# Self-attention: the value product of the first half of the keys in three split terms, and the value bias added where attended values leave PSUM

## The reference, cut to what matters

```
q = (h @ wq + bq), k = (h @ wk + bk), v = (h @ wv + bv)      # 16 heads of 128
q = q * cos + _rotate_half(q) * sin                          # k alike
scores = jnp.einsum('bhqd,bhkd->bhqk', q, k) / math.sqrt(HD)
scores = jnp.where(causal[None, None], scores, jnp.finfo(jnp.float32).min)
probs = jax.nn.softmax(scores.astype(jnp.float32), axis=-1).astype(q.dtype)
out = jnp.einsum('bhqk,bhkd->bhqd', probs, v)
return out.transpose(0, 2, 1, 3).reshape(b, s, H * HD) @ wo + bo
```

## Time and profile before

| | us |
|---|---|
| median of three runs | 1918.01 |
| profiled execution | 1916.59 |
| span of its trace | 1914.5 |
| mean granted TensorE clock | 0.962 of full |
| busy: TensorE / ScalarE / VectorE / GpSimd | 1746.0 / 1314.5 / 1090.2 / 1069.3 |
| the self-attention stage, about | 418 to 1012 |

### The profile page before, as it was taken

One profiled execution on the slowest core, in us unless ns is written; L12 is line 12 of the kernel. 1 busy time (PEld: TensorE's weight loads), 2 busy tenths in 40 slices (PEclk: granted clock), 3 DMA queues, 4 the chain that ended last, 5 costly groups with the idle time before them and its releaser, 6 DMA issues.

```text
span 1914.5 us, 36598 instructions
## 1 busy us (share of the span) xinstructions
PE 1746.0 (91%) x11648; PEld 1571.9 (82%) x11648; DVE 1090.2 (57%) x3109; ACT 1314.5 (69%) x4238; POOL 1069.3 (56%) x1187
## 2 busy tenths in 40 slices
PE   4499999449999999999998997999999999999798
PEld 1388888338999999999987885888888888888797
DVE  1477777556666666566775555455555555565222
ACT  1277778248888888888884443788888888888221
POOL 1433334379988889889962113444544544554364
PEclk9699999759999999999998998999999999999899
DMA  3000001110000000000002000000000000000000
GB/s 113 23 17 18 15 21 34 53 33 12 18 23 12 18 23 12 18 18 12 18 7 77 19 28 7 8 12 11 8 12 8 11 12 11 20 14 14 4 23 23
DMA packets 28384, 40.23 MB, mean 21 GB/s; under 512 B 4770, under 2 KB 18338, under 8 KB 27940
## 3 DMA queue, kind: packets, MB, share of 16 engines
q1 hardware_dynamic: 28196, 37.90, 6.6%
HBM read 33.69 MB, written 4.19 MB: 20 GB/s over the span
## 4 chain that ended last, share of the span: by engine, by line
PE 68%; ACT 13%; issue 5%; POOL 4%; DVE 4%; DMA 1%; POOLq 0%; SPq 0%; ACTq 0%; DVEq 0%
PE pS L947 4%; PE pF L508 4%; PE pF L510 4%; PE pF L509 4%; ACT pA L1562 4%; PE pA L510 3%; PE pA L509 3%; PE pA L508 3%; PE pA L939 3%; PE pA L938 3%; PE pA L940 3%; PE pO L966 3%; PE pF L679 3%; PE pS L658 3%; ACT x_P L1588 2%
## 5 line engine op out<-in xcount | busy, mean ns | idle before, releaser
L508 PE MATMUL pA<-Wh,XTh 128*128 128x512 f32 (+1 forms) x512 | 221.5, 433 | 5.6 <-DVEq L117 2.9
L1310 POOL TENSOR_TENSOR f_sw<-f_sw,f_sin 128x512 f32<-128x512 f32 x128 | 179.9, 1406 | 40.6 <-ACT f_sw L1059 40.6
L510 PE MATMUL pA<-Wh,XTl 128*128 128x512 f32 (+1 forms) x512 | 188.7, 369 | 0.0
L509 PE MATMUL pA<-Wl,XTh 128*128 128x512 f32 (+1 forms) x512 | 188.6, 368 | 0.0
L1059 ACT ACTIVATE f_sw<-pA 64x512 f32<-64x512 f32 x256 | 152.0, 594 | 37.3 <-PE pA L940 33.5
L938 PE MATMUL pA<-XTh,Wh 128*128 128x256 f32 x512 | 163.1, 319 | 10.9 <-DMA wg<-in_w_gate 10.3
L1313 POOL TENSOR_TENSOR f_sw<-f_sw,f_RB 128x512 f32<-128x512 f32 x128 | 166.9, 1304 | 10.0
L1588 ACT ACTIVATE x_P<-x_P,x_nm 128x192 f32<-128x192 f32 (+1 forms) x256 | 128.8, 512 | 35.8 <-DVE x_nm L1704 35.8
L503 POOL TENSOR_TENSOR Wl<-RAW,Wh 128x256 fp32r<-128x256 f32 (+3 forms) x64 | 61.0, 952 | 159.9 <-ACT Wh L496 159.9
L939 PE MATMUL pA<-XTl,Wh 128*128 128x256 f32 x512 | 145.4, 284 | 0.0
L940 PE MATMUL pA<-XTh,Wl 128*128 128x256 f32 x512 | 145.3, 284 | 0.0
(11 more groups left out here) (275 smaller groups left out, 6093.7 us busy)
## 6 DMA issues: line engine op xcount, KB each, us to landing
RAW<-in_w_f SPq DMA_DIRECT2D x32, 256.0 KB, 2.7
RAW<-in_w_x SPq DMA_DIRECT2D x32, 160.0 KB, 2.2
RAW<-in_w_x SPq DMA_DIRECT2D x32, 128.0 KB, 2.0
RAW<-in_w_ff SPq DMA_DIRECT2D x8, 288.0 KB, 2.8
R<-in_x SPq DMA_DIRECT2D x4, 512.0 KB, 5.9
x_spill<-R SPq DMA_DIRECT2D x1, 2048.0 KB, 7.5
RAW<-in_w_moe SPq DMA_DIRECT2D x8, 256.0 KB, 2.6
moe_xs<-x_spill SPq DMA_DIRECT2D x8, 256.0 KB, 3.1
```

The costliest lines, as they stand in the source:

```text
L508: e.matmul(o, ah, bh, start=first, stop=False)
L509: e.matmul(o, ah, bl, start=False, stop=False)
L510: return e.matmul(o, al, bh, start=False, stop=last)
L1310: e.tensor_tensor(y, y, bc(sind[:, :], 1, 2), ALU.mult).then_inc(q["swm"], 1)
```

## The change

The value product over the first 128 keys is done as three split products, in place of one float32 product; the one over the last 128 keys stays as it is. For that the probabilities of those keys (PTh, PTl) and V of the first 128 positions (Vh, Vl) are kept as high and low parts. ScalarE's `p_ev` becomes two copies (PTh with 256 columns, PT1 with 128). VectorE gets a new step `p_low` for each head, which makes PTl from pT and PTh; `take(i,4)` becomes a copy to Vh and a subtraction to Vl, `take(i,5)` a plain copy. `attend` now waits for pl, raised by `p_low`, and no longer for te. The bias of V is added in `o_ev` and `o_low`, from a table bv of one column for each head that is loaded once ahead of the stage instead of four broadcast loads.

```diff
@@ attend (TensorE)
-                    e.wait_ge(q["te"], at_p(i, h) + 1)
+                    e.wait_ge(q["pl"], HG * i + h + 1)
...
-                    e.matmul(pO[:, 0:S], V[:, i % 2, 0, v], PT[:, h % 2, 0:S], start=True, stop=False)
-                    e.matmul(pO[:, P:S], V[:, i % 2, 1, v], PT[:, h % 2, S:S + P], start=False, stop=True
+                    three(e, pO[:, 0:S], Vh[:, i % 2, v], Vl[:, i % 2, v], PTh[:, h % 2, :], PTl[:, :], True, False)
+                    e.matmul(pO[:, P:S], V1[:, i % 2, v], PT1[:, h % 2, :], start=False, stop=True
                              ).then_inc(q["pv"], 1)
@@ p_tr (TensorE); norm_tr and logits get the same wait
                     e.wait_ge(q["te"], pos(c - 1))
+                    if c >= 2:
+                        e.wait_ge(q["pl"], lows(c))
@@ p_ev and o_ev (ScalarE)
-                    e.activation(PT[:, h % 2, :], pT[:, c % 2, 0:SW], ACT.Copy).then_inc(q["te"], 1)
+                    e.activation(PTh[:, h % 2, :], pT[:, c % 2, 0:S], ACT.Copy)
+                    e.activation(PT1[:, h % 2, :], pT[:, c % 2, S:SW], ACT.Copy).then_inc(q["te"], 1)
...
-                    e.activation(OTh[:, i % 2, h, :], pO[:, 0:S], ACT.Copy).then_inc(q["oth"], 1)
+                    x = (i // 8) * HG + h
+                    e.activation(OTh[:, i % 2, h, :], pO[:, 0:S], ACT.Identity, bias=bv[:, x:x + 1]
+                                 ).then_inc(q["oth"], 1)
@@ take, n = 4 and 5 (VectorE)
-                        e.tensor_tensor(V[:, i % 2, n - 4, :], pA[:, n % 2, :], bv[:, g % 2, :], ALU.add
+                        if n == 5:
+                            e.tensor_copy(V1[:, i % 2, :], pA[:, n % 2, :]).then_inc(q["taken"], 1)
+                            return
+                        e.tensor_copy(Vh[:, i % 2, :], pA[:, n % 2, :]).then_inc(q["vh"], 1)
+                        e.wait_ge(q["vh"], i + 1)
+                        e.tensor_tensor(Vl[:, i % 2, :], pA[:, n % 2, :], Vh[:, i % 2, :].bitcast(F32), ALU.subtract
                                         ).then_inc(q["taken"], 1)
@@ o_low and p_low (VectorE)
-                    e.tensor_tensor(OTl[:, i % 2, h, :], pO[:, 0:S], OTh[:, i % 2, h, :].bitcast(F32),
-                                    ALU.subtract).then_inc(q["ot"], 1)
+                    x = (i // 8) * HG + h
+                    e.scalar_tensor_tensor(OTl[:, i % 2, h, :], pO[:, 0:S], bv[:, x:x + 1],
+                                           OTh[:, i % 2, h, :].bitcast(F32), ALU.add, ALU.subtract
+                                           ).then_inc(q["ot"], 1)
+
+                def p_low(i, h):
+                    c = at_p(i, h)
+                    e.wait_ge(q["te"], c + 1)
+                    e.wait_ge(q["pv"], HG * i + h)
+                    e.tensor_tensor(PTl[:, :], pT[:, c % 2, 0:S], PTh[:, h % 2, :].bitcast(F32), ALU.subtract
+                                    ).then_inc(q["pl"], 1)
@@ VectorE's list of an iteration
                     soft(i, 2)
+                    p_low(i, 0)
                     w_high(i)
...
                         take(j, 3)
                         take(j, 4)
+                    p_low(i, 1)
                     w_low(i)
...
                         soft(j, 0)
+                    p_low(i, 2)
...
                         recip(j, 1)
+                    p_low(i, 3)
```

More of the change, by code:

```diff
@@ L859, in self_attention @@
             bqk = sb(name + "_bqk", [P, 4, NH], F32, scope)
-            bv = sb(name + "_bv", [P, 2, GW], F32, scope)
+            bv = sb(name + "_bv", [P, NH], F32, scope)
             RB = sb(name + "_RB", [P, 2, 2 * NT, S], F32, scope)
@@ L864, in self_attention @@
             kT = sb(name + "_kT", [P, 2, HG, S], F32, scope)
-            V = sb(name + "_V", [P, 2, T, GW], F32, scope)
+            Vh = sb(name + "_Vh", [P, 2, GW], F32R, scope)
+            Vl = sb(name + "_Vl", [P, 2, GW], F32R, scope)
+            V1 = sb(name + "_V1", [P, 2, GW], F32, scope)
             PB = sb(name + "_P", [P, HG, SW], F32, scope)
@@ L869, in self_attention @@
             rs = sb(name + "_rs", [P, HG, T], F32, scope)
-            PT = sb(name + "_PT", [P, 2, SW], F32, scope)
+            PTh = sb(name + "_PTh", [P, 2, S], F32R, scope)
+            PTl = sb(name + "_PTl", [P, S], F32R, scope)
+            PT1 = sb(name + "_PT1", [P, 2, P], F32, scope)
             OTh = sb(name + "_OTh", [P, 2, HG, S], F32R, scope)
@@ L876, in self_attention @@
             names = ("nhi", "nlo", "raw0", "raw1", "hi", "split", "proj", "taken", "sw", "swm", "swb", "rb", "rope", "tr", "te", "sc", "sct",
-                     "ex", "rs", "pn", "pv", "oth", "ot", "f", "acc", "const", "bias0", "bias1")
+                     "ex", "rs", "pn", "pv", "oth", "ot", "f", "acc", "const", "pl", "vh")
             q = {x: sem(f"{name}_{x}") for x in names}
             raw_in = [q["raw0"], q["raw1"]]
-            bias_in = [q["bias0"], q["bias1"]]
             turns = []
@@ L892, in at_p, with lows @@
                 return place["p", i, h]
+            def lows(c):
+                return sum(x[0] == "p" for x in turns[:c - 1])
             def sp(e):
@@ L897, in sp @@
                 e.dma_start(mask[:, :], d["mask_f0"]).then_inc(q["const"], 16)
+                e.dma_start(bv[:, :], d["f0_bv"]).then_inc(q["const"], 16)
                 e.dma_start(bqk[:, :, :].rearrange("p a n -> p (a n)"), d["f0_bqk"]).then_inc(q["const"], 16)
                 e.dma_start(wg[:, :, :].rearrange("p k e -> p (k e)"), d["w_gate"]).then_inc(q["const"], 16)
[L901 to L905, removed]
                 for i in range(NI):
                     g = i // 8
-                    if i % 8 == 1 and g < G - 1:
-                        e.wait_ge(q["taken"], NQ * 8 * g)
-                        biases(g + 1)
                     if g == G - 1:
@@ L995, in logits @@
                     ins.then_inc(q["tr"], 1)
-                e.wait_ge(q["const"], 80)
+                e.wait_ge(q["const"], 96)
                 for n in range(NQ):
@@ L2519, in layout @@
                                        rows(a[f0 + "wo"][g * GW:(g + 1) * GW])], 1) for g in range(G)])
-    o["f0_bv"] = a[f0 + "bv"]
+    o["f0_bv"] = col(a[f0 + "bv"])
     bqk = np.concatenate([col(a[f0 + "bq"]), col(a[f0 + "bk"])], 1)
```

2 lines of the change are left out of this document (removed).

## The result

| | before | after |
|---|---|---|
| median of the runs, us | 1918.39 (1918.01 to 1922.36, 4 runs) | 2078.82 (2077.20 to 2081.00, 4 runs) |
| profiled execution, us | 1916.6 | 2078.91 |
| its span, us | 1914.5 | 2077.1 |
| mean granted TensorE clock | 0.962 | 0.942 |

The change makes the kernel slower: ratio 1.0832 (95% interval 1.0813 to 1.0851). Forecast: 2066, range 2013 to 2096.

A forecast was written before the change was run, and what follows sets the result against it. The self-attention stage was taken to run at TensorE's own pace (busy 182.00 of 182.00 us). 1916.6 - 9.7 + 81.5 + 36.6 + 4 + 0.5 = 2029.5, with 1.4 to the median 2031, plus 35 for the clock 2066; range 2013 to 2096.

The forecast's parts named there:

- Head 1: Value product waits for p_low behind take(j,3), take(j,4); T is its transposes' start; stall 2.63 us, 81.5 over 31 iterations.
- Head 3: Value product waits for p_low behind recip(j,1), which waits for ScalarE's exp; stall 1.18 us, 36.6 over 31 iterations.
- Heads 0 and 2, reserve 0.15, no stall: p_low right behind a softmax pass ends at T + 2.16 to 2.21, product due at T + 2.4.
- TensorE's saving, 9.7 us: Three split products of 0.118 us replace a 0.43 step: 0.076 us a head, 9.7 over 128 heads.
- The clock, 21 x 1.7 = 35 us: TensorE's clock falls behind head 1's gap in two of three iterations, 1.7 us each; bounds 0 and 53.
- Rival B: Both stalls come but TensorE's clock holds: 2031 us (2012 to 2045), chance 0.32.
- Late iterations, +4: From iteration 25 VectorE's row statistics and another pass stand ahead of p_low(i,3): about 4 us in all.
- Start, +0.5: One more DMA issued ahead of the constants' wait, 0.43 us, put at 0.5 in the sum.
- The bias at nothing: Adding V's bias when pO is emptied costs nothing: same elements, and both steps come after the product.
- The 1.4 that was added from the profiled execution to the median: The median of the runs is 1.4 us above the profiled execution, so 2029.5 becomes 2031.

The follow-up runs named there:

- e2_h1: The changed kernel with only p_low(i,1) moved up to right behind soft(i,3): 1962.22 us, ratio 1.0230 to the kernel before.
- e3_h3: The changed kernel with only p_low(i,3) moved up to right behind soft(j,1): 2064.74 us, ratio 1.0757 to the kernel before.
- e1_both: The changed kernel with p_low(i,1) moved up behind soft(i,3) and p_low(i,3) behind soft(j,1): 1951.96 us, ratio 1.0169 to the kernel before.
- e12_p1: e6_s0 with w_high moved behind recip(j,0), w_low behind add_out, and p_low(i,1) ahead of soft(i,3): 1927.29 us, ratio 1.0048 to the kernel before.
- e8_fill: The changed kernel with ten useless 256-column products on TensorE ahead of head 1's wait: 2048.62 us, ratio 1.0695 to the kernel before.
- e4_bias: The kernel before with only V's bias moved into the two steps that empty pO: 1920.46 us, ratio 1.0007.
- e6_s0: e1_both with VectorE's list around head 0 reordered and ScalarE's swapped(j,2) put behind p_ev(i,0): 1943.55 us, ratio 1.0146 to the kernel before.

## Why the prediction was right, step by step

- **Head 1.** Product at T + 4.90 forecast, T + 4.96 measured. The stall, counted as the prediction does with the late first result, was put at 2.63 and is 2.70 (8.45 - 5.83, and the 0.08 that the products save). The order on VectorE was as described; e2_h1 shows that its place is the cause.
- **Head 3.** T + 3.49 forecast, T + 3.44 measured. Its size was right (1.18 forecast, 1.14 measured in the same way), its independence was not: taken away alone (e3_h3) it gives 14 us and only 0.12 in a steady iteration, since head 0 is next.
- **Heads 0 and 2, reserve 0.15, no stall.** Right for the kernel after (2.43 and 2.41). The reserve of head 0 was that of a stretched iteration, though: with head 3 prompt it was short by 0.74. My expectation for e1_both fell on it.
- **TensorE's saving, 9.7 us.** In the steps it is there (3.00 against 3.08 behind head 0, 5.86 against 5.91 behind head 2). With the long waits gone (e12_p1) none of it is left in the iteration: at head 0 it is lost to ScalarE's normalise, at heads 1 and 3 to starts 0.06 and 0.08 late.
- **The clock, 21 x 1.7 = 35 us.** About 34 (21.6 + 12), at most some 5 more, of which e8_fill gave back 30. The rows gave 1.7 a fall and it was 1.54; falls in 15 of iterations 0 to 26 instead of two in three, and longer ones in 27 to 30. That the total fits is in part luck. The count came from a line drawn between two gaps, and it set the stall of 2.63 beside idle times; the idle time that the rows show is 2.43, less than half of the way from 2.01 to 2.88. Rival B, no fall, is refuted for this kernel. The Trainium skill, "TensorE: Matmul & The Clock Gate", part on the HAM clock gate, has as its practical rule to keep idle gaps under a length that is greater than 2.43 us; the trace does not agree that this is enough, since 2.43 us of idling was followed by 1.2 GHz in every second iteration.
- **Late iterations, +4.** The one term that was clearly mis-sized: 24.6 us beyond the steady waits, some 12 of it the clock's, so about 13 where 4 was put (with 1.7 of iteration 0). I counted VectorE's row statistics ahead of p_low(i,3), and not ScalarE's normalisation copies ahead of p_ev(i,1), which bring 0.91 more at head 1 (5.87 against 4.96), nor that head 3 went from 3.44 to 4.66.
- **Start, +0.5.** Measured +1.9, within the scatter of the kernels with the same start, and +4.5 behind the last head, where nothing was put: 0.9 of waiting, and most of the rest by the look of it one more fall of the clock. Neither was tested apart.
- **The bias at nothing.** Right to within 2 or 3 us (e4_bias), though both operations are longer than what they replace, by 0.09 and 0.06 us.

The sum came out 13 us low: about 9 in the late iterations and 6 at the start and the end, the rest of the terms within 2 of what was put. The 1.4 that was added from the profiled execution to the median did not come (2078.91 and 2078.82).

## What to carry to other kernels

When a change puts a small operation of another engine between two steps of the bound engine, the price is not its length but what stands ahead of it in that engine's queue, and what those wait for: 0.42 us cost 2.7 and 1.1. Price each such wait from the row order, but do not add up what mending them would give, since a wait in front is the reserve of the one behind. And a gap of two to three microseconds on TensorE can have a second price, its clock; work put into the gap, even useless work, can be cheaper than the gap.

## What the runs showed of the hardware

The clock behind equal gaps alternated: 2.43 us idle, then 1.2 GHz for some 3 us in one iteration and none in the next, over the iterations 3 to 26. A gap of about 0.87 at head 3 alone never brought it down in iterations 1 to 24 (e2_h1, a clock of 1.00 from 438 to 966).

Two of VectorE's passes from SBUF to SBUF, the cast and the subtraction of the weights, take longer beside GpSimd. The same cast of 128x512 took 0.42 us in the kernel after and 1.45 in e6_s0; its companion, the subtraction of L503, took 1.66 in the one, where GpSimd's pass under way had 1.11 left, and 0.71 in the other, where it had 0.15 left. Where the cast began 0.06 us ahead of GpSimd's pass (e1_both), GpSimd's took 1.49 instead of 1.28 and the cast 0.42:

```profile
704.63 0.42 DVE L1236 CAST Wh<-RAW 128x512 fp32r<-128x512 f32 x1
```

```profile
704.69 1.49 POOL L1333 TENSOR_TENSOR f_sw<-f_sw,f_sin 128x512 f32<-128x512 f32 x1
```

Who came second took longer. The Trainium skill, "SBUF — State Buffer", section "SBUF: two separate sides", says that the two engines share a pair of ports that is held for a whole instruction; the rows agree with it.

A bias costs on either engine: ScalarE's eviction of 128x256 from PSUM took 475 ns with one and 381 as a plain copy, VectorE's subtraction 477 with the bias, as another instruction, and 416 without. In e4_bias it was 471 and 478.
